# Moving the last routing round, the last lists and the tile plan under the first shared-expert tiles, and spreading a routing round over eight heads

## The reference

```python
def _L0_xattn_ref(k, v, q, ssm_kernel, D, head_dim):
    kv = jnp.einsum('bhil,bhjl->bijhl', k_, v_)
    ...
    out = y + kv * D[None, None, None, :, None]      # y: kv convolved along l with the head's kernel
    out = jnp.einsum('bijhl,bhil->bjhl', out, q_)
...
logits = x.astype(jnp.float32) @ router_w.astype(jnp.float32)
scores = jax.nn.sigmoid(logits)
scores_grouped = (scores + router_bias).reshape(T, G, E // G)
top2, _ = jax.lax.top_k(scores_grouped, 2)
group_scores = top2.sum(-1)
_, top_groups = jax.lax.top_k(group_scores, TKG)
...
_, top_k_index = jax.lax.top_k(masked, K)
tkw = jnp.take_along_axis(scores, top_k_index, axis=-1)
tkw = tkw / tkw.sum(-1, keepdims=True)
...
routed = (down[unsort].reshape(T, K, H) * tkw[..., None]).sum(axis=1)
shared = jax.nn.silu(x @ sw_gate) * (x @ sw_up) @ sw_down
...
x = x + _L0_xattn_ref(ctx_2048, ctx_2048, _layernorm(x, axis=-1), L0_xattn_ssm_kernel, L0_xattn_D, 8)
x = x + _L0_ffn_ref(_layernorm(x, axis=-1), ...)
```

## Time and profile before

| | |
|---|---|
| median of 3 runs | 13609.86 us (13609.02 to 13610.19) |
| the profiled execution's own time | 13610.97 us |
| its span, first to last instruction | 13609.1 us |
| TensorE busy | 13142.6 us, 97% of the span |
| VectorE, ScalarE, GpSimd busy | 5798.7, 3143.2, 6330.1 us |
| mean granted TensorE clock | 0.986 |
| stage 1 ends, plan ends | about 2258.6 us, 2349.2 us |

### The profile page before, as it was taken

How to read it: one execution, slowest core, us unless ns; L and a number is a source line. 1 busy time by engine, 2 the same in 40 slices (tenths; PEclk the granted TensorE clock), 3 DMA queues, 4 the chain that set the end, 5 groups by cost and what they waited for, 6 DMA issues and landing times.

```text
span 13609.1 us, 192445 instructions
## 1 busy us (share of the span) xinstructions
PE 13142.6 (97%) x59424; PEld 10914.0 (80%) x59425; DVE 5798.7 (43%) x6513; ACT 3143.2 (23%) x4072; POOL 6330.1 (47%) x6629
## 2 busy tenths in 40 slices
PE   8999995999999999999999999999898999999999
PEld 7888884888888888877888887877787888888887
DVE  6888785333333333343333333333334333333333
ACT  4444442111122111222122212222222112112111
POOL 5688886111444444444444444444444444444111
PEclk9999997999999999999999999999999999999999
DMA  3333333444444444455455545555555444444444
GB/s 120 118 115 111 115 115 91 135 128 127 113 114 110 103 107 104 115 146 127 98 114 132 115 97 127 125 135 142 141 115 159 98 97 114 97 97 103 128 128 120
DMA packets 876587, 1597.96 MB, mean 117 GB/s; under 512 B 169537, under 2 KB 518081, under 8 KB 850306
## 3 DMA queue, kind: packets, MB, share of 16 engines
q0 software_dynamic: 258560, 642.82, 23.1%
q1 hardware_dynamic: 134018, 600.31, 13.2%
q10 hardware_dynamic: 483840, 352.54, 10.4%
HBM read 995.66 MB, written 599.86 MB: 117 GB/s over the span
## 4 chain that ended last, share of the span: by engine, by line
PE 76%; DMA 2%; DVE 2%; issue 1%; ACT 1%; ACTq 0%; DVEq 0%; SPq 0%; POOL 0%
PE gps L1274 26%; PE ups L1274 26%; PE yps L1274 25%; DMA hsd<-hb 1%; DVE wlo L1199 1%; DMA hz<-hsd 1%; DMA raw<-in_w_gu_dram 0%; ACT whi L1143 0%; ACT xhi L1149 0%; DVE xlo L1199 0%; DVEq L991 0%; ACTq L1155 0%; DVE hp L1232 0%; ACTq L991 0%; DVE hb L1234 0%
## 5 line engine op out<-in xcount | busy, mean ns | idle before, releaser
L1112 POOL DMA_INDIRECT x2d<-yrow,yidx x544 | 945.7, 1738 | 3837.2 <-issue 1581.8
L1076 POOL DMA_INDIRECT xg<-xnd,xidx x2176 | 2156.7, 991 | 969.0 <-issue 473.2
L1199 DVE TENSOR_TENSOR xlo<-xt,xhi 128x1024 fp32r<-128x1024 f32 x672 | 822.5, 1224 | 3792.3 <-ACT xhi L1149 3792.3
L1274 PE MATMUL gps<-whi,xhi 128*128 128x512 f32 x5376 | 2098.2, 390 | 211.4 <-DVE xlo L1199 119.1
L1274 PE MATMUL ups<-whi,xhi 128*128 128x512 f32 x5376 | 2094.1, 390 | 0.0
L1274 PE MATMUL gps<-wlo,xhi 128*128 128x512 f32 x5376 | 2093.7, 389 | 0.0
L1274 PE MATMUL ups<-wlo,xhi 128*128 128x512 f32 x5376 | 2093.4, 389 | 0.0
L1274 PE MATMUL gps<-whi,xlo 128*128 128x512 f32 x5376 | 2093.3, 389 | 0.0
L1274 PE MATMUL ups<-whi,xlo 128*128 128x512 f32 x5376 | 2093.1, 389 | 0.0
L1274 PE MATMUL yps<-whi,hhi 128*128 128x512 f32 x5376 | 1667.6, 391 | 124.4 <-DVE wlo L1199 116.7
L1274 PE MATMUL yps<-wlo,hhi 128*128 128x512 f32 x5376 | 1662.3, 390 | 0.0
(11 more groups left out here) (149 smaller groups left out, 17382.3 us busy)
## 6 DMA issues: line engine op xcount, KB each, us to landing
hsd<-hb ACTq DMA_DIRECT2D x2688, 64.0 KB
hz<-hsd ACTq DMA_DIRECT2D x672, 256.0 KB, 2.7
raw<-in_w_gu_dram SPq DMA_DIRECT2D x136, 1024.0 KB, 7.2
raw<-in_w_dn_dram SPq DMA_DIRECT2D x68, 1024.0 KB, 6.9
xg<-xnd POOLq DMA_DIRECT2D x512, 128.0 KB
yrow<-x2d SPq DMA_DIRECT2D x128, 512.0 KB, 3.4
kT<-in_ctx_dram SPq DMA_DIRECT2D x64, 704.0 KB, 8.1
xg<-xnd,xidx POOLq DMA_INDIRECT x2176
```

Source lines behind the costliest of these rows:

```text
L1076: pool.indirect_dma_start(out=xg[i][:, q, :], out_offset=None, in_=quarters, in_offset=bass.IndirectOffsetOnAxis(ap=xidx[i][:, q:q + 1], a ...
L1112: pool.indirect_dma_start(out=acc, in_=yrow[i][:, :], in_offset=None, out_offset=bass.IndirectOffsetOnAxis(ap=yidx[i][:, 0:1], axis=0), co ...
L1199: return dve.tensor_tensor(dst, src, hi.bitcast(F32), ALU.subtract)
L1274: ins = pe.matmul(ps, rows, w[:, chunk, i * 512:(i + 1) * 512], start=first and n == 0, stop=last_one and n == 2)
```

## The change

It does five things.

1. A round's VectorE work becomes eight pieces: `group_scores`, `choose_groups`, `choose`, `weigh` in steps 4 to 7 of one block of steps and `count`, `order`, `match`, `hand_over` in steps 0 to 3 of the next. The compare products of `assign` are made in two halves, four tiles each, in `match` and `hand_over`. TensorE's `ranks` moves to step 7. GpSimd writes a round's 64 entries as 11 in each of steps 4 to 7 and 10 in steps 0 and 1.
2. Stage 1 ends with the last sigmoid. The last round's eight pieces and `plan_tiles` are done by VectorE in shared tiles 2 to 7 and 18 to 20, each between the sum of the rows and hlo; TensorE's two rank matmuls stand in tile 5.
3. GpSimd writes the lists of the last two rounds during shared tiles, four entries per tile (from tile 0 on, and from tile 20 on), each after `x_turned`. The rows of the first 64 tiles are loaded by SyncE (`load_rows`, `pass_on`).
4. Stage 2 is gone. Expert 0's weights are loaded at the start of the feed-forward, behind the rows of tile 0, and the first unit is split before the low part of x. SyncE stores and loads the table after tile 24.
5. `xres` has two buffers; constants, scores and counts are kept for both stages.

```diff
-LOOPED = (2, 7)
+LOOPED = (3, 7)
...
+SHARES = [range(0, 11), range(11, 22), range(22, 33), range(33, 44), range(44, 54), range(54, 64)]
...
+    def match_half(h):
+        s = slice(h * RB // 2, (h + 1) * RB // 2)
+        shape = [P, RB // 2, K, E]
+        link(dve.tensor_tensor(wide, key[:, s, :].rearrange("p t (o e) -> p t o e", o=1).to_broadcast(shape),
+                               top[:, s, :].rearrange("p t (k o) -> p t k o", o=1).to_broadcast(shape),
+                               ALU.is_equal))
+        link(dve.tensor_tensor(wide, wide, wn[:, s, :].rearrange("p t (o e) -> p t o e", o=1).to_broadcast(shape),
+                               ALU.mult))
+        link(dve.tensor_reduce(pair[:, s, :, :].bitcast(F32)[:, :, :, 1], wide, AXX, ALU.add))
+
+    def match(r):
+        dve.wait_ge(place_free, r + 1)
+        match_half(0)
...
-                if isinstance(s.block, int) and s.block == BLOCKS - 1:
-                    list_tokens(s.block - 2, (2 * s.u, 2 * s.u + 1))
-                elif s.u < 7 and routes(s, s.u, 2):
-                    list_tokens(s.block - 2, ((0,), (1,), (2,), (3,), (4,), (5,), (6, 7))[s.u])
-                elif routes(s, 7, 2):
-                    free_place(s.block - 2)
+                for u in range(4, 8):
+                    if routes(s, u, 2):
+                        list_tokens(s.block - 2, SHARES[u - 4])
+                for u in range(2):
+                    if routes(s, u, 3):
+                        list_tokens(s.block - 3, SHARES[4 + u])
+                if routes(s, 2, 3):
+                    pool.wait_ge(listed, 16 * RB * K * (s.block - 2))
+                    pool.sem_inc(place_free, 1)
...
+                for u in range(4, 8):
+                    if routes(s, u, 1):
+                        route[u - 4](s.block - 1)
+                for u in range(4):
+                    if routes(s, u, 2):
+                        route[u + 4](s.block - 2)
...
-                    pe.wait_ge(rank_used, s.block + int(s.u > 5))
+                    wait(pe, rank_used, s.block)
...
+            load_rows(0, 0)
+            load_weights(sp, raw, w_ld, *expert_weights(A, 0), lambda unit: None)
+            load_rows(1, 1)
+            for i in range(2):
+                fetch(i, i)
+            load_rows(2, 0)
             load_weights(sp, raw, w_ld, *expert_weights(A, 1), before_unit(1))
-            sums(store_half, half_st)
+            pass_on(store_half, half_st, 0, PLANNED + 4, 3)
+
+            sp.wait_ge(tab_ready, 1)
...
+            for n in range(0, RB * K, 4):
+                pool.wait_ge(x_turned, 2 + n // 4)
+                settle(pool, pool_turns)
+                list_some(pool, lists, pair, place, range(n, n + 4), listed[0])
+            pool.wait_ge(listed[0], 16 * RB * K)
+            pool.sem_inc(place_free, 1)
+            pool.wait_ge(placed, 1)
+            for n in range(0, RB * K, 4):
+                pool.wait_ge(x_turned, PLANNED + 2 + n // 4)
+                settle(pool, pool_turns)
+                list_some(pool, lists, pair, place, range(n, n + 4), listed[1])
...
-            split_gu(0)
+            split_gu(0, range(1))
             x_high(0)
-            walk_tiles(act, tile)
+            split_gu(0, range(1, GU))
+            walk_first(act, tile)
...
+                if c.piece is not None:
+                    (route + (plan_tiles,))[c.piece](0)
                 if c.on():
                     dve.wait_ge(h_hi, t + 1)
```

More of the change, by code:

```diff
@@ L176, in settle, with list_some @@
     pool.sem_inc(turns, 1)
-def list_tile(pool, lists, pair, place, t, listed):
-    for k in range(K):
+SHARES = [range(0, 11), range(11, 22), range(22, 33), range(33, 44), range(44, 54), range(54, 64)]
+def list_some(pool, lists, pair, place, share, listed):
+    for n in share:
+        t, k = n // K, n % K
         pool.indirect_dma_start(
@@ L241, in mix_and_route @@
         lg = sb("lg", [P, RB, E])
[L242 to L245, removed]
         chosen = sb("chosen", [P, RB, E])
         wn = sb("wn", [P, RB, E])
[L248 to L258, removed]
+        work = sb("work", [P, WORK])
+        con, biasb, sc, cnt, tokf = (keep[k] for k in ("con", "biasb", "sc", "cnt", "tokf"))
         pair, place = keep["pair"], keep["place"]
@@ L683, in _ @@
+            route = routing(dve, link, chosen, wn, work, pss[:, 0:2 * RB * E], keep,
+                            (scored, chose, rank_mm, rank_used, place_free, placed))
             dve.sem_inc(rank_used, 1)
@@ L700, in _ @@
             walk(dve, step, seq)
-            choose_groups(NTILE // RB - 1)
-            choose(NTILE // RB - 1)
-            count(NTILE // RB - 1)
-            assign(NTILE // RB - 1)
         @block.tensor
@@ L919, in on, with pairs, walk_first, walk_rest @@
         return not self.fixed or 0 <= self.n(k) < TILES
-PHASES = ((0, R0), (R0, R1), (R1, TILES))
-def walk_tiles(eng, tile):
+PIECES, RANKS, CHOSEN = 9, 3, 6
+PLANNED = 20
+def pairs(eng, tile, first, end):
+    with eng.Fori(0, (end - first) // 2) as turn:
+        for u in range(2):
+            tile(Tile(first, u, turn))
+def walk_first(eng, tile):
     for t in range(2):
         tile(Tile(t))
-    for first, end in PHASES:
-        with eng.Fori(0, (end - first - 6) // 2) as turn:
-            for u in range(2):
-                tile(Tile(first + 2, u, turn))
+    for u in range(CHOSEN):
+        tile(Tile(2 + u, piece=u))
+    pairs(eng, tile, 2 + CHOSEN, PLANNED - 2)
+    for u in range(CHOSEN, PIECES):
+        tile(Tile(PLANNED - PIECES + 1 + u, piece=u))
+    tile(Tile(PLANNED + 1))
+    pairs(eng, tile, PLANNED + 2, R0 - 4)
+def walk_rest(eng, tile):
+    for t in range(R0 - 4, R0 + 2):
+        tile(Tile(t))
+    for first, end in ((R0, R1), (R1, TILES)):
+        pairs(eng, tile, first + 2, end - 4)
         for t in range(end - 4, min(end + 2, TILES + 1)):
@@ L1039, in _, with load_rows, pass_on @@
-            load_weights(sp, raw, w_ld, *expert_weights(A, 1), before_unit(1))
-            sums(store_half, half_st)
+            def load_rows(n, i):
+                wait(sp, x_turned, n - 1)
+                rows = xnd[bass.ds(n * P, P), :].rearrange("(q s) (a l) -> a s q l", q=QUADS, a=QUADS)
+                for a in range(QUADS):
+                    sp.dma_start(xg[i][a * SQ:(a + 1) * SQ, :, :], rows[a]).then_inc(half_x_ld[i], 16)
+            def pass_on(store, stored, first, end, ahead=0):
+                with sp.Fori(0, (end - first) // 2) as turn:
+                    for i in range(2):
+                        n = first + 2 * turn + i
+                        if ahead:
+                            load_rows(n + ahead, (i + ahead) % 2)
+                        store(n, i)
+                        sp.wait_ge(stored[i], 16 * (first // 2 + turn + 1))
+                        fetch(n + 2, i)
@@ L1044, in _ @@
                 sp.wait_ge(y_st[i], 16 * EXPERT_TILES // 2)
-            sums(store_sum, out_st)
+            for i in range(2):
+                fetch(i, i)
+            pass_on(store_sum, out_st, 0, NTILE - 2)
+            for i in range(2):
+                store_sum(NTILE - 2 + i, i)
             for i in range(2):
@@ L1118, in tile @@
                     load_list(c, 3)
-                if c.on(2):
+                if c.on(2) and c.part(2) != 0:
                     bring(c, 2)
```

419 lines of the change are left out of this document (203 added, 216 removed).

## The result

The changed kernel took 13453.25 us (median of 4 runs, 13449.4 to 13456.75), the kernel before 13610.01 us beside it; the ratio is 0.9884 [0.9872, 0.9895]. The prediction was 13450. The profiled execution took 13453.46 us, with a span of 13451.6 and a mean clock of 0.991, where 0.986 was before. Against the span before, 13609.1, that is 157.5 us less; the prediction's sum said 159.4.

A forecast was written before the change was run, and what follows sets the result against it. TensorE, busy 97%, bounds the kernel; only its idle or half-clock stretches count. 112.4 (seam) + 0 (first tiles) + 48 (spreading) - 1 (rank matmuls) = 159.4 off 13610.97 gives 13451.6, forecast 13450 us; 80% range 13436 to 13505.

The forecast's parts named there:

- The seam: Between first stage and feed-forward: the feed-forward opens at 2236.8 instead of 2349.2 us, a gain of 112.4 us.
- rival 1: First stage: stalls move to `match` or the router matmul instead of vanishing; gain there 15 to 25 us; chance 0.14.
- The first tiles: Start of the feed-forward, with expert 0's weights now loading there: between 3.6 us gained and 15 lost, taken as 0.
- the path of h: Feed-forward's start: the next steps wait for h's write and read, not the first matmul, so 0 was taken.
- The first matmul: Start of the feed-forward: it comes 13 us after the opening, where the old kernel needed 16.7 us.
- The rows of tile 1: SyncE's queue: they land behind 6 MB of weights, about 17 us later, before tile 0's matmuls end; sum unchanged.
- The spreading: First stage, routing cut into eight pieces: gain 48 us, between 20 (half the stalls come back elsewhere) and 52.
- `count` before the router's matmul: First stage, step 0: `count` ends at 1657.8 us, TensorE's third group at 1657.9 with eight transposes before that matmul.
- What went under shared tiles: Shared tiles: pieces, list writes, row loads and table cost nothing; two rank matmuls cost 1 us, once.
- Rival 2: Shared tiles: list writes slow the path of h, 51 us over 32 tiles (13501), fewer tiles 13470; chance 0.12.
- Rival 3: 63 shared tiles: SyncE's circle, put at 14.4 us, sets the pace; 63 us at 17.3; chance 0.05, 0.03 slower.
- Rival 4: Start of routed tiles: lists or table come late and the seam stays there, leaving 13561 us; chance 0.02.

The follow-up runs named there:

- e3: The changed kernel with expert 1's weights loaded during shared tiles 40 to 50, not behind the rows of tile 2: 13462.56 us, ratio 0.9839.
- e4: The changed kernel with the first list writes held three tiles later, until tile 3's rows are turned: 13465.81 us, ratio 0.9842.
- e1: The changed kernel with the first stage's pieces, ranks and list writes put back in their old places, new seam kept: 13508.51 us, ratio 0.9872.
- e2: The changed kernel with `order`, `match` and `hand_over` all in step 3, not steps 1, 2 and 3: 13492.04 us, ratio 0.9862.
- e7: The changed kernel with a 512 KB load and a wait for it added to SyncE's circle in 60 shared tiles: 13622.44 us (one run).
- r3: The kernel before, unchanged, profiled on the third chip of the experiments: 13696.36 us.
- e5: The changed kernel with the 64 list writes of each of the last two rounds in one burst, not four per tile: 13603.45 us, ratio 0.9935.
- r2: The kernel before, unchanged, profiled on the second chip of the experiments: 13705.05 us.

## Why the prediction was right

- **The seam, 112.4 us.** Right: the next stage opens 0.3 us behind the last sigmoid, and what that opening gained beyond 112.4 is put down to the first stage. Its working has a slip of 0.2 us: 2236.3 and 0.3 are 2236.6, not 2236.8. (Two more slips change nothing: 42.9 + 10 is 52.9, not 52, and a gain of 15 to 25 in rival 1 gives 13473 to 13483.)
- **The first tiles, taken as 0.** The one clearly mis-sized term on the chip of the result: 8.9 us lost, inside the stated bound of 15. The sentence "the next steps wait for the path of h" pointed at the place, but the price beside it was none. The first matmul came as said (12.4 us, said 13). The rows of tile 1 landed behind the weights, as the prediction had it, near 2211 us, 18 to 20 us behind their issue and some 1.6 us before tile 0's gate and up matmuls ended. What fails is to count the early first matmul as safe: TensorE then waits 10.3 us for a write of h that meets expert 1's loads and the first list writes (e3, e4).
- **The spreading, 48 us.** Measured 50.5, with 1.1 us of product waits left. `count` before the router's matmul did cost something, 4.3 us in all, as its margin under 1 us let one fear. e1 and e2 show that the stalls are the placement's. The clock's share fits too: up to 2150 us TensorE was busy at the lower clock for 30.1 us before and for 10.2 us now; 20 us less of that are 10 us of time, as said. On another chip the gain is 26.6 us, near the low end of 20, and the stalls did not come back elsewhere as that end supposed; in part it is "issue" gaps.
- **What went under shared tiles.** Pieces, plan, table and lists cost 0.5 us at most behind the first tiles of this trace, the rank matmuls 0.9, predicted 1. In four runs on two other chips 2.4 to 7 us are lost behind the table, which the prediction put at nothing.
- **Rival 1**, stalls that move: 4.3 us of new waits, not 25. **Rival 2**, list writes that slow the path of h: in the first tiles they do, together with 4 MB of weights (e3, e4); in the steady ones the path became shorter (7.5 us, was 9.0), but for the three tiles behind the table on other chips. What they slow there is SyncE's fetch and row loads, 1.5 to 1.7 times, under the circle's slack. The Trainium skill ("DMA: Bandwidth & Descriptors", Specifications) has transfers under 512 B below line rate and as a read-modify-write; the trace agrees that such writes weigh far more than their 0.06 MB, but from 2580 to 2800 us their packets take only 0.7% of the 16 engines' time, so by which way they slow the others no run tells. **Rival 3**, the circle: 13.7 us in e7 without its addition and beside list writes, predicted 14.4; it has 2.6 us to spare, and it holds. **Rival 4** didn't occur.
- **Missed gain.** The hand-over to the routed tiles, 4 us, was in no step. It and the spreading's 2.5 us made up for most of the first tiles' loss of 8.9. That the sum is 2 us off and not 9 is luck.

## What to carry to other kernels

Work that waits behind a stage's end is worth its full length if the next stage has an engine with a pause in each step; measure that pause and cut the work into pieces shorter than it. At the new seam, count not the first matmul but the first result that must pass through HBM, and keep bulk loads and small writes away from it. Don't issue dozens of indirect transfers in a row beside running engines: four to eleven at a time cost no stop, 64 all but stopped TensorE, VectorE and ScalarE on two of the chips.

## What the runs showed of the hardware

- On the second and third chip of the experiments, a run of 64 indirect writes of 128 x 8 bytes, 1.27 us apart, let TensorE start one matmul per 2.80 us (r3, e5) or wait 59.8 us for VectorE (r2). VectorE stood still for 53 to 77 us, ScalarE for up to 69 (e5). It began some 15 us (r2), 18 and 21 us (e5) and 30 us (r3) into the burst and ended 7 to 10 us after the last write was issued. On the first chip the same writes did nothing of the kind.
- Chips differ by stage: the same kernel before took 13610 us on one and 13681 to 13692 us on others, and in the two profiled executions that run so, 81 and 88 us lay in the first stage, 65 and 74 of them beside the burst of list writes. The same first stage of the changed kernel ended at 2186.0 us on the first chip and at 2206.6 to 2217.5 on others. So the change is worth 157 us on one chip and 206 on another, and on a third the burst alone costs the kernel before 63.
- The write of h (four transfers of 64 KB) landed 1.4 us behind its issue in a later tile, 3.6 in the first tile with list writes beside it (e3), 9.1 with 4 MB of expert 1's weights (e4), and 14 with both.
- Four list writes per tile, 0.06 MB in 14 tiles, lengthen SyncE's fetch of 512 KB from 3.9 to 6.6 us; the read of h, on ScalarE's queue, takes 2.7 us beside them and 3.8 without.
